# Attention scores by key from float16 halves, and row statistics from accumulated sums and ScalarE squares

## The reference

```
q = layernorm(x) @ Wq ; k = ctx @ Wk ; v = ctx @ Wv        # 16 heads of 32
q, k = rope(q), rope(k)
score = q k^T / sqrt(32) ; attn = softmax(score)
x = x + (attn @ v) @ Wo
h = act_qdq(layernorm(x))                                   # one scale for the whole tensor
up, gate = act_qdq(h @ Wup^T), act_qdq(h @ Wgate^T)          # 4-bit weights in blocks of 32
x = x + act_qdq(gate * sig(gate) * up) @ Wdown^T
```

## Time and profile before

| | us |
|---|---|
| three runs | 2293.67, 2294.55, 2299.99 |
| median | 2294.55 |
| span of the profiled execution | 2290.3 |
| median less span | 4.25 |
| PE busy | 2195.0 (96%) |
| DVE busy | 1689.5 (74%) |
| ACT busy | 1329.6 (58%) |
| POOL busy | 708.0 (31%) |

### The profile page before, as it was taken

One profiled execution on the slowest core, in us unless ns is written; L12 is line 12 of the kernel. 1 busy time (PEld: TensorE's weight loads), 2 busy tenths in 40 slices (PEclk: granted clock), 3 DMA queues, 4 the chain that ended last, 5 costly groups with the idle time before them and its releaser, 6 DMA issues. The chain is left out here.

```text
span 2290.3 us, 31254 instructions
## 1 busy us (share of the span) xinstructions
PE 2195.0 (96%) x12081; PEld 971.8 (42%) x12081; DVE 1689.5 (74%) x1696; ACT 1329.6 (58%) x1299; POOL 708.0 (31%) x655
## 2 busy tenths in 40 slices
PE   6998999999998999999999999999996899999999
PEld 3443333333333444444444444444443344444444
DVE  7757998898976666555532798888888787777773
ACT  3446666666654233223322978787876777778772
POOL 3645666666654211001100454343443000000000
PEclk9999999999999999999999999999998899999999
DMA  6444777777855677888775998777875466565552
GB/s 196 108 122 128 183 186 184 192 184 190 181 156 177 195 233 234 262 255 270 255 225 184 323 328 301 277 282 288 298 281 228 184 239 234 216 239 212 203 210 92
DMA packets 287191, 500.14 MB, mean 218 GB/s; under 512 B 187981, under 2 KB 190285, under 8 KB 250173
## 3 DMA queue, kind: packets, MB, share of 16 engines
q1 hardware_dynamic: 287036, 498.10, 67.9%
HBM read 247.75 MB, written 186.58 MB: 190 GB/s over the span
## 5 line engine op out<-in xcount | busy, mean ns | idle before, releaser
L1721 PE MATMUL banks<-XB,W 128*128 128x512 f16 x2304 | 498.1, 379 | 1.1 <-ACT XB L1747 0.8
L1721 PE MATMUL banks<-XB,WT 128*128 128x512 f16 x2304 | 497.4, 379 | 0.0
L2191 PE MATMUL banks<-W,OH 128*128 128x512 f16 x2256 | 488.7, 380 | 2.8 <-DVE OH L2297 2.8
L1741 ACT ACTIVATE OB<-banks,uns 128x512 f32<-128x512 f32 x384 | 255.4, 683 | 391.2 <-PE banks L1721 385.3
L1721 PEld LDWEIGHTS banks<-XB,W 128*128 128x128 f16 x2304 | 224.8, 98 | 274.1 <-DVE XB L1780 1.9
L1721 PEld LDWEIGHTS banks<-XB,WT 128*128 128x128 f16 x2304 | 225.1, 98 | 272.2
L2191 PEld LDWEIGHTS banks<-W,OH 128*128 128x128 f16 x2256 | 220.7, 98 | 270.6 <-DVE OH L2297 3.5
L2013 POOL TENSOR_TENSOR PR<-GS,OB 128x2048 f32<-128x2048 f32 x46 | 220.3, 4790 | 257.8 <-ACT OB L1741 247.8
L1830 DVE TENSOR_REDUCE amx<-OB 128x1 f32<-128x2048 f32 x48 | 109.7, 2285 | 237.6 <-ACT OB L1741 237.6
L770 PE MATMUL banks<-XC,AH 128*128 128x512 f16 x768 | 176.0, 380 | 8.4 <-POOL AH L1533 3.3
L711 PE MATMUL banks<-XD,WQ 128*128 128x512 f16 x768 | 177.0, 380 | 2.1 <-ACT QE L1021 0.8
(11 more groups left out here) (276 smaller groups left out, 2897.0 us busy)
## 6 DMA issues: line engine op xcount, KB each, us to landing
g_s<-OB SPq DMA_DIRECT2D x48, 1024.0 KB, 6.0
GL<-g_s SPq DMA_DIRECT2D x48, 1024.0 KB, 7.6
up_s<-OB SPq DMA_DIRECT2D x48, 1024.0 KB, 4.9
XA<-up_s SPq DMA_DIRECT2D x32, 1024.0 KB, 9.4
gq_s<-GQ SPq DMA_DIRECT2D x48, 512.0 KB, 4.9
XD<-gq_s SPq DMA_DIRECT2D x48, 512.0 KB, 6.7
XA<-in_x SPq DMA_DIRECT2D x16, 1024.0 KB, 6.3
QW<-QE SPq DMA_DIRECT2D x128, 128.0 KB, 3.1
```

Source lines behind the costliest of these rows:

```text
L1721: t = e.matmul(pk[:].rearrange("p (j t) -> p j t", j=4), WT[w][:, ot, wa, kk, :], XB[i % 2][:, xa, :, kk, :], start=(kk == 0 and wa == 0 a ...
L1741: e.activation(OB[n % 3][:, r, :], bank[(k + 4) % 8][:], ACT.Copy, scale=uns[:, 12 * w + ot:12 * w + ot + 1]).then_inc(s_ev, 1)
L2191: t = e.matmul(pk[:].rearrange("p (r n) -> p r n", r=4), OH[i % 2][:, a, ot, j * 128:(j + 1) * 128], WD[:, :, c, wa, o4, :], start=(ot == ...
```

## The change

1. The rotated queries and keys are kept as two float16 tensors, a high and a low part, where there was one float32. `pe_scores` multiplies three pairs of parts (high by high, high by low, low by high): 12 float16 matmuls for four float32 ones. `pe_largest` takes the high parts for all units; `act_half` is gone.
2. The rotation is now done in place: the cosines are multiplied into QE itself, and therefore wait for the DMAs that read QE. DVE adds QW into QE. Then ACT writes the high part (`act_rope_high`) and POOL the low part (`pool_rope_low`), of each of the 80 tiles (64 of queries, 16 of keys). QE has five buffers to tile 25 and four after it; a buffer is free when the low part is done.
3. The unit of the weights and of the context goes into the scale of the exponential; QE is written with fixed steps.
4. For the first 48 output tiles the statistics are done otherwise: DVE's residual instruction also accumulates the row sum, one 128x1 instruction makes the mean of it, ACT squares `x - mean` with an accumulated sum (`act_square`), over the buffer of the residual, and DVE takes the largest square after the maxima (`dve_x1_largest`). The instructions L1226 and L1232 and their aggregates are gone for these tiles; L1231 has a counterpart. The residual's buffer now holds the squares, so the next load of it waits for that largest, and is issued behind the swap.

```
-            for g in range(4):
-                e.matmul(PB[0:SK, g, :], KR[g0][32 * g:32 * g + 32, c, bb * SK:(bb + 1) * SK], QR[u % 8][32 * g:32 * g + 32, :],
-                         start=True, stop=False)
+            e.wait_ge(s_rlo, ROT["q", u] + 1)
+            e.wait_ge(s_rlo, ROT["k", 8 * g0 + c] + 1)
+            for n, (ka, qa) in enumerate(((0, 0), (0, 1), (1, 0))):
+                for g in range(4):
+                    e.matmul(PB[0:SK, g, :], KR[g0][32 * g:32 * g + 32, ka, c, bb * SK:(bb + 1) * SK],
+                             QR[u % NQ][32 * g:32 * g + 32, qa, :], start=(n == 0), stop=False)
...
+def halves_at(s):
+
+    if s < 2:
+        return [0, 1] if s == 0 else [2, 3, 4]
+    return tiles_at(s - 1) if s <= NU else []
...
         def act_rope_in(e, n):
-            if n >= 4:
...
+            if n >= 5:
+                e.wait_ge(s_rlo, qe_before(n) + 1)
+
+        def act_rope_high(e, n):
+
+            what, i = ROTS[n]
             e.wait_ge(s_radd, n + 1)
...
+            if what == "q" and i >= NQ:
+                e.wait_ge(s_c1, i - NQ + 1)
+            e.activation(rot_half(n, 0), qe(n)[:, 0:rot_width(n)], ACT.Copy).then_inc(s_rhi, 1)
...
+        def act_square(e, u):
+
+            xr, x1, _, _ = x_of(u)
+            e.wait_ge(s_st2, mean_done(u))
+            if u:
+                e.wait_ge(s_st2, range_done(u - 1))
+            e.activation(xr, x1, ACT.Square, bias=mv2[:, u, 0:1], accum_out=mv2[:, u, 1:2]).then_inc(s_sq2, 1)
...
-                if HALF <= s - 1 < NU:
-                    act_half(e, s - 1)
+                for n in halves_at(s) if s != 1 else []:
+                    act_rope_high(e, n)
+                for u in output_at(s - 1):
+                    if u < 4 * BY_SUM:
+                        act_square(e, u)
...
+            if u < 4 * BY_SUM:
+                mean = mv2[:, u, 0:1]
+                e.scalar_tensor_tensor(x1, o_bank(u), vun[:, 2:3], xr, ALU.mult, ALU.add, accum_out=mean).then_inc(s_x1, 1)
+                e.wait_ge(s_x1, u + 1)
+                e.tensor_scalar(mean, mean, -1.0 / D, None, ALU.mult).then_inc(s_st2, 1)
+                return
...
+        def dve_x1_largest(e, u):
+
+            xr, _, _, _ = x_of(u)
+            e.wait_ge(s_sq2, u + 1)
+            e.tensor_reduce(rs2[:, u // 4, 4 + u % 4:5 + u % 4], xr, AX.X, ALU.max).then_inc(s_st2, 1)
...
+            elif u < 4 * BY_SUM + 2:
+                e.wait_ge(s_st2, range_done(u - 2))
...
+                if 2 <= s - 16 < LATE:
+                    sp_xr_load(e, s - 16)
...
+            to = qe(n)[:, 0:rot_width(n)]
+            e.tensor_tensor(to, to, QW[n % 2][:, 0:rot_width(n)], ALU.add).then_inc(s_radd, 1)
...
+            e.wait_ge(s_qw[n % 2], 32 * (n // 2 + 1))
+            e.tensor_tensor(v(qe(n)), v(qe(n)), cc, ALU.mult)
...
+        def pool_rope_low(e, n):
+
+            e.wait_ge(s_rhi, n + 1)
+            e.tensor_tensor(rot_half(n, 1), qe(n)[:, 0:rot_width(n)], rot_half(n, 0), ALU.subtract).then_inc(s_rlo, 1)
...
                 for u in normal_at(s):
                     pool_normal(e, u)
+                for n in halves_at(s):
+                    pool_rope_low(e, n)
                 if s < NU:
                     pool_rope_cosine(e, ROT["q", s])
```

More of the change, by code:

```diff
@@ L288, in build @@
         cq, sq = sbuf(st, "cq", [128, 512]), sbuf(st, "sq", [128, 512])
-        KH = [W0[:, 12000 + SK * i:12000 + SK * (i + 1)] for i in range(2)]
         ck, sk = (W0[:, 11520 + 2 * SK * i:11520 + 2 * SK * (i + 1)].bitcast(FP32) for i in range(2))
@@ L360, in x_of, with mean_done, range_done @@
             return xr, x1, i, 16 * (m + 1 + (LATE // 2 if i < 2 else 0))
+        def mean_done(u):
+            return 2 * u + 1 if u < 4 * BY_SUM else 3 * u + 1 - 4 * BY_SUM
+        def range_done(u):
+            return 2 * u + 2 if u < 4 * BY_SUM else 3 * u + 3 - 4 * BY_SUM
         def rr(b):
@@ L917, in act_rope_in @@
         def act_rope_in(e, n):
-            if n >= 4:
-                before = n - 4 if n < 6 else n - 2
-                e.wait_ge(s_rm1, before + 1)
-                e.wait_ge(s_qw[n % 2], 32 * (before // 2 + 1))
-                what, u = ROTS[before]
-                if what == "q" and u >= HALF:
-                    e.wait_ge(s_sm, u + 1)
-        def act_half(e, u):
-            g0, bb = divmod(u // 4, 4)
-            n = ROT["q", u]
-            e.wait_ge(s_radd, n + 1)
-            e.wait_ge(s_rm1, n + 1)
-            e.wait_ge(s_qw[n % 2], 32 * (n // 2 + 1))
-            if u >= HALF + 2:
-                e.wait_ge(s_sm, u - 1)
-            e.activation(KH[u % 2], KR[g0][:, u % 4, bb * SK:(bb + 1) * SK], ACT.Copy, scale=1.0 / QS)
-            e.activation(qh(u), QR[u % 8][:], ACT.Copy, scale=1.0 / QS).then_inc(s_half, 1)
+            if n >= 5:
+                e.wait_ge(s_rlo, qe_before(n) + 1)
+        def act_rope_high(e, n):
+            what, i = ROTS[n]
+            e.wait_ge(s_radd, n + 1)
+            if what == "q" and i >= NQ:
+                e.wait_ge(s_c1, i - NQ + 1)
+            e.activation(rot_half(n, 0), qe(n)[:, 0:rot_width(n)], ACT.Copy).then_inc(s_rhi, 1)
         def act_kv(e, i):
@@ L943, in act_kv @@
                 e.wait_ge(s_k, 4 * g + r + 1)
-                e.wait_ge(s_cu, 4 * g + 3)
                 act_rope_in(e, n)
-                e.activation(qe(n)[:, 0:4 * SK], bank[kv_bank(i)][:, 0:4 * SK], ACT.Copy, scale=cun[:, g, 2:3]).then_inc(s_qe, 1)
+                e.activation(qe(n)[:, 0:4 * SK], bank[kv_bank(i)][:, 0:4 * SK], ACT.Copy, scale=K_STEP).then_inc(s_qe, 1)
             else:
@@ L975, in act_largest @@
                 e.wait_ge(s_c1, 4 * (b - 1) + 4)
-            e.activation(MT[:], BQ_, ACT.Copy, scale=(QS * QS if 4 * b >= HALF else 1.0) / MS).then_inc(s_mte, 1)
+            e.activation(MT[:], BQ_, ACT.Copy, scale=1.0 / MS).then_inc(s_mte, 1)
         def act_attention(e):
@@ L2409, in _tables @@
     tok = (4 * np.arange(128)[None, :] + np.arange(4)[:, None]).reshape(-1)
-    f = np.float32(QS)
-    cq = cos[tok][:, half].T * f
-    sq = sin[tok][:, half].T * sign[:, None] * f
-    ck = cos[:SK][:, half].T * f
-    sk = sin[:SK][:, half].T * sign[:, None] * f
+    cq = cos[tok][:, half].T
+    sq = sin[tok][:, half].T * sign[:, None]
+    ck = cos[:SK][:, half].T
+    sk = sin[:SK][:, half].T * sign[:, None]
     return [np.ascontiguousarray(a.astype(np.float32)) for a in (cq, sq, ck, sk, np.eye(128))]
```

173 lines of the change are left out of this document (94 added, 79 removed).

## The result

The changed kernel takes **2332.09 us** (median of 4 runs, 2331.56 to 2334.85) against 2296.25 for the kernel before (4 runs): a ratio of 1.0167, 95% interval 1.0155 to 1.018. It is slower by 35.8 us by the two medians, and by some 38 us by the ratio; the forecast was 2300, with a range to 2320. The profiled span grew from 2290.3 to 2332.7 us. That is 42.4 us, more than the medians differ by: the profiled execution of the changed kernel is the longest of its four (2334.85), and a recorded execution takes 1.7 to 3.0 us more than its span, so part of the 4.25 us that I had put outside the span of the kernel before only says that its profiled execution was a fast one.

What follows compares the result with a forecast made beforehand. Stalls of PE in attention were taken to end in a chain through POOL and the DMAs; 2290.3 of span + 11 (start) - 5 (steady part) - 1 (tail) + 4.25 outside gave 2300 us, range 2272 to 2320 (8 in 10).

Steps and rivals of the forecast that it cites:

- Scores by key: PE's scores by key in each unit: 0.71 us in place of 0.96, 0.25 saved, bounds 0 and 0.27.
- The start: Attention up to 222 us: 20.5 us of delays less PE's gains and old stalls, +11 us, bounds 0 and +17.
- Lower bound 0, if the five buffers let ACT run ahead: Start: it costs nothing if QE's five buffers let ACT run ahead; with two, ACT had also waited for DMAs.
- Against it stand the gains of PE [...] 8.4 us, and about 1 us of old stalls: Start, from step 6: PE saves 0.77 in 8 steps and 0.25 in 9; about 1 us of old stalls disappear.
- The steady part: Steps 16 to 63, 222 to 676 us: -5 us, with ends of -34 and +15.
- I take 0: Steady part, eight groups set by the chain through POOL: between -1 and +1.3 us a group, taken as 0.
- DVE's relief at almost nothing: Statistics, late groups: taking some 1.9 us from in front of the maxima on DVE is worth almost nothing.
- The tail: Steps 64 on: eight scores at 0.25 us saved, half of them hidden, -1 us.
- the first: Rival: DVE and PE set the time after all, the maxima's stalls go; about 2277 us, chance 0.29.
- The second: Rival: POOL becomes the bound, steady part +14 in place of -5; 2319 us, chance 0.19.
- The third: Rival: the 12 matmuls of 32 rows run one after another, +1.8 us in 64 units; 2410 us, chance 0.02.
- The shared ports: DVE and POOL lock the same SBUF ports: 80 low parts make more adds wait; unsummed, time as in The second.

Runs made afterwards that it cites:

- start_order2: Changed kernel; in steps 0 to 5 ACT makes key tiles' high parts behind its evacuations, POOL low parts behind the step's cosines and sines: 1.0098, 2317.41 us.
- cos_twice: Kernel before, with each cosine product of the rotation done twice on POOL (80 more products), nothing else of the change: 1.0096, 2317.17 us.
- start_dve: start_order2 with the low parts of steps 6 to 15 made on DVE in place of POOL: 1.0137, 2322.85 us.
- dve_low_all: Changed kernel with DVE in place of POOL making the low part of each rotated tile from step 3 on: 1.0169.
- loop_start: start_order2 with sums one step earlier from step 16, reciprocal rows' load ahead of the residual's, fourth context's largest ahead of step 5's adds: 1.0233.
- keys_only: Changed kernel without its statistics part (BY_SUM = 0), float16 halves kept: 1.0182, 2335.93 us.
- loop_before: Kernel before, with the sums of the exponentials copied and sent through DRAM one step earlier from step 16 on: 0.9945, 2279.79 us.
- loop_after2: Changed kernel with the sums of the exponentials one step earlier from step 16, reciprocal rows' load left behind the residual's: 1.0131, 2321.19 us.
- stats_only: Kernel before with the statistics part of the change alone, without float16 halves: 1.0014, 2297.27 us.

## Why the prediction was wrong

- **Scores by key**: right. 0.69 us in place of 0.96; step 17 now lasts 8.58 us, 8.84 before.
- **The start**: +25.9 us for +11. Its first half was right in kind and too small. Late were the queries of step 4 by 9.7 us (82.9, forecast 79 to 81.5), step 5 by 16.1 (10.5 by my terms), step 6 by 22.2 (16.5), step 8 by 27.0 (20.5 less the gains to there). The waits that I had named came: 4.6 us of PE for a key tile's evacuation in step 4 (3.5 by my terms), 3.7 for ACT's values in step 5 (6), 5.1 for a key tile's in step 7 (4). What I had not walked is the fifth buffer. "Lower bound 0, if the five buffers let ACT run ahead" turned out the other way round: it binds the sixth tile's evacuation to the first tile's low part, 5.1 us of PE in step 2. start_order2, which began step 6 at 97.9 us, shows all this to be order. The step that failed by most is the other half, "Against it stand the gains of PE [...] 8.4 us, and about 1 us of old stalls". PE's busy time to step 16 rose by 1.7 us in place of falling by 8.4, at a granted clock of 0.89 for 0.95, and its idle time rose by 24.2 (19.5 by my terms). From step 9 (26.1 us late) to step 16 (25.9) nothing was repaid, where the terms promise 5.6. I had priced the gains at the clock of before.
- **What of the start stays open**: the 12 us that start_order2 leaves, all behind step 6. cos_twice shows that as much more work on POOL can cost 13.6 us in the order of before; start_dve and dve_low_all show that handing it to DVE gives nothing back. Two waits are named, of steps 6 and 7; loop_start shortened the first and did not gain by it.
- **The steady part**: +8.2 us to the first matmul of step 64's output projection (675.97 before, 710.04 after), for -5. "I take 0" for the chain through POOL in eight groups was the step that failed. I had the first low part (1.27) and the later cosines, but left out the 128x8 power (1.64 for 1.01) and the low part's time beside DVE: 2.14 at 456.03, while DVE's two-input instructions on XA run from 455.25 to 459.25, where another (430.81) takes 1.15. Above all I left out that the chain can close into a loop, so that PE's saving of 0.27 a step counts nowhere. keys_only (427.8) and cos_twice (428.7) against 418.0 show the price of the halves and of POOL's work. loop_before shows the loop in the kernel before, loop_after2 that it accounts for about 10 us in the changed one. The rest of the wait there is POOL's stretch behind the load of the rows, by the traces alone.
- **DVE's relief at almost nothing**: right, and stats_only (1.0014) shows it.
- **The tail**: +8.3 for -1; it was not walked. One wait for POOL, and a projection at a lower clock behind it, make 6.2 us of it (the kernel before waited 3.27 us there, and its projection took 2.75):

```profile
741.42 5.20 PE L805 MATMUL banks<-XC,AH 128*128 128x512 f16 x12 [7.01 <-POOL AH L1596]
```

  The low parts are not all of it, since stats_only and loop_before, which have none, also lost 3.7 and 3.6 us behind step 60.
- **The rivals**: the first is excluded by the waits for the maxima, which did halve and gave nothing. The second has the nearest sum, 2319, and its +14 for the steady part lies further off than the +8.2 measured; groups took 38.8 us, not over 39.5. The third is excluded by the 0.69 us.
- **The shared ports**: the adds did not get slower (1145 ns in the mean, 1172 in the earlier trace rows); it was the low parts that did, 1367 ns in the mean of the steady part. So the time came near the second rival's, but not by the way of the rule.
- **The range** ended at 2320. The start alone passed its own upper bound (+25.9 for +17); the steady part stayed inside its own (+15), and the tail of 8.3 had none. The lower end of the steady part was also summed wrongly: 24 and 48 x 0.25 are 36, not 34; nothing hung on it.

## What to carry to other kernels

Follow a stall's chain until it leaves the group of steps, not to the first busy engine. If it returns to itself one group later, the period is the sum of its latencies, and work taken off one engine need not show in the time: in the kernel before, DVE's relief gave nothing, while the sums put one step earlier gave 0.55%. Then look for the next chain, since the same edit left the wait in the changed kernel. When a buffer is freed by a later product than before, walk the first tiles that reuse it, each evacuation that stands in line behind it too. Don't book work saved on an engine as time saved in a stretch where it waits, and where its clock may come out lower. Before a load is moved ahead of another on one queue, look at what lands behind it.

## What the runs showed of the hardware

A load of 256 KB that SyncE issued right behind two row broadcasts of 256 KB each was used only 7.9 us after its issue (386.37 to 394.29), where the median from issue to landing of such loads in the kernel before, from 250 to 640 us, is 4.8 us (last number):

```profile
RX<-in_x SPq DMA_DIRECT2D x41, 256.0 KB, 4.8
```

The Trainium skill says in "DMA: Bandwidth & Descriptors", section "Two DMAs through the same engine are not ordered", that within one queue of one DMA engine descriptors start in order. These numbers fit that, but don't show it: one place on the queue went with 3 us more to the landing, and whether by order, by the broadcasts' traffic or by other traffic of that moment, no run tells apart. Further, a gap of 2.3 us on PE was at times followed by a projection of 4.42 us and at times by one of 2.76, in the same place of the loop; gaps of up to 1.7 us in steps 16 to 63 of the kernel before were never followed by the slow one.
